# A four-part graph kernel on one core: pad rows only where they are read, block counts early in the table, gathers eight groups ahead, and edge rows inside the adding loop

## The reference, cut to what matters

```python
# relational layer, twice: one matrix of 20 per edge type, built from 8 bases
W   = jnp.einsum('rb,bio->rio', a, V)
seg = dst * R + etypes
agg = jax.ops.segment_sum(x[src], seg, num_segments=N * R).reshape(N, R, -1)
h   = jnp.einsum('nri,rio->no', agg, W) + x @ w_loop + bias
# plain sum
out = jax.ops.segment_sum(x[src], dst, num_segments=N)
# flow layer: a two-layer MLP per edge, forwards and backwards
fwd = mlp([x[future], x[past], edge_attr]);  fwd_agg = segment_sum(fwd, future)
bwd = mlp([x[past], x[future], edge_attr]);  bwd_agg = segment_sum(bwd, past)
out = mlp([fwd_agg, bwd_agg])
# attention over the edges of a node, 4 heads of 8
```

## Time and profile before

| what | us |
|---|---|
| runs | 3404.99, 3411.47, 3412.61 |
| median | 3411.47 |
| the profiled execution | 3402.48 |
| its span | 3400.5 |
| sort, to its last scatter | 843.2 |
| adding loop's stage | 851 to 986.5 |
| message table again, second relational layer | 986.5 to 1484 |
| sum layer | 1484 to 1889 |
| flow layer's pipeline | 1889 to about 2650 |
| attention | 2717 to 3400 |

### The profile page before, as it was taken

The page is one execution under the profiler, slowest core; times in us unless marked ns, Lnnn a source line. Parts: engine busy times, 40 slices in busy tenths (PEclk is TensorE's granted clock), DMA queues, the critical chain, the costliest instruction groups (busy, mean ns, idle before and its releaser), DMA issues. The chain is left out here.

```text
span 3400.5 us, 58425 instructions
## 1 busy us (share of the span) xinstructions
PE 2791.8 (82%) x19728; PEld 1844.5 (54%) x19838; DVE 2957.7 (87%) x8386; ACT 653.1 (19%) x1566; POOL 2125.8 (63%) x2076
## 2 busy tenths in 40 slices
PE   5788889885669999969998799999999767777752
PEld 3455555553446777746665466666666533333321
DVE  5999999996857999979999688888888479999987
ACT  2110101100310000001111222222222133333320
POOL 0377777776005777757775677777775277777740
PEclk6798988987556888869999799999999778888875
DMA  9111111110412111121111100000001011111120
GB/s 256 58 35 35 34 36 35 34 36 21 132 60 72 25 25 24 19 25 28 29 29 19 16 11 11 11 11 11 11 11 9 11 27 27 27 28 27 27 16 5
DMA packets 133363, 116.09 MB, mean 34 GB/s; under 512 B 58505, under 2 KB 116941, under 8 KB 132957
## 3 DMA queue, kind: packets, MB, share of 16 engines
q0 software_dynamic: 65152, 44.96, 8.4%
q1 hardware_dynamic: 64332, 59.23, 7.0%
q10 hardware_dynamic: 3600, 8.19, 0.7%
HBM read 70.58 MB, written 41.65 MB: 33 GB/s over the span
## 5 line engine op out<-in xcount | busy, mean ns | idle before, releaser
L1628 POOL DMA_INDIRECT flow_x<-node_table,src_indices x440 | 539.3, 1226 | 228.9 <-issue 104.5
L706 PE MATMUL p_in_picked<-block_table 128*96 128x512 bf16 x1725 | 446.1, 422 | 106.4 <-DVE block_table L594 106.4
L594 DVE TENSOR_SCALAR block_table<-in_sources,node_numbers 128x512 bf16<-128x512 f16 x1725 | 520.0, 371 | 0.8 <-PE p_in_picked L706 0.6
L1998 POOL DMA_INDIRECT att_kv_rows<-kv_table,att_index x440 | 425.1, 966 | 141.4 <-issue 132.2
L1086 POOL DMA_INDIRECT rel_rows<-message_table,message_indices x320 | 322.7, 1008 | 300.2 <-POOLq L1303 203.0
L1770 PE MATMUL flow_acc_bwd<-flow_onehot_j,flow_by_q 128*128 128x270 bf16 (+1 forms) x2530 | 493.7, 325 | 7.1 <-issue 0.2
L414 POOL DMA_INDIRECT sorted_edges<-block_table,sorted_row x416 | 406.3, 977 | 147.8 <-issue 147.8
L706 PEld LDWEIGHTS p_in_picked<-block_table 128*96 128x96 bf16 x1725 | 229.5, 136 | 297.2 <-DVE block_table L594 93.6
L1379 POOL DMA_INDIRECT sum_rows<-node_table,src_indices x280 | 270.4, 966 | 111.3 <-issue 85.0
L2034 DVE TENSOR_REDUCE att_tile_max<-p_att_scores 128x4 f32<-128x512 f32 x440 | 284.2, 684 | 28.4 <-PE p_att_scores L2148 24.9
L1414 DVE TENSOR_SCALAR sum_source_onehot<-sum_sources,node_numbers 128x512 bf16<-128x512 f16 x1000 | 300.6, 367 | 0.0
(11 more groups left out here) (344 smaller groups left out, 4997.7 us busy)
## 6 DMA issues: line engine op xcount, KB each, us to landing
sorted_edges<-pad_rows SPq DMA_DIRECT2D x1, 11440.0 KB, 54.7
rel_rows<-sorted_edges SPq DMA_DIRECT2D x20, 572.0 KB, 3.8
in_sources<-source_rows_in SPq DMA_DIRECT2D x69, 128.0 KB
message_table<-message_rows ACTq DMA_DIRECT2D x25, 320.0 KB, 2.2
message_table<-message_rows SPq DMA_DIRECT2D x25, 320.0 KB, 2.1
flow_x<-node_table,src_indices POOLq DMA_INDIRECT x440
att_kv_rows<-kv_table,att_index POOLq DMA_INDIRECT x440, 2.5
sorted_edges<-block_table,sorted_row POOLq DMA_INDIRECT x416, 2.2
```

Of the source, the lines that this page charges most:

```text
L594: last = dve.tensor_scalar(which[g % 2][:, c, :], srcs[b][:], s["node"][:, c:c + 1], None, ALU.is_equal)
L706: last = pe.matmul(pp[g % 2][0:3 * F, 0:CW], hs[:, c].rearrange("p k f -> p (k f)"), which[g % 2][:, c, :], start=(c == 0), stop=(c == NB ...
L1628: pool.indirect_dma_start(out=X[b][:, t, 0:F], out_offset=None, in_=d["nodes"], in_offset=bass.IndirectOffsetOnAxis(ap=s["idx_src"][:, g * ...
L1998: pool.indirect_dma_start(out=KV[b][:, t, :], out_offset=None, in_=d["kv"], in_offset=bass.IndirectOffsetOnAxis(ap=ibuf[b][:, t:t + 1], ax ...
```

## The change

Six edits, in program order:

1. Pad rows are written by SyncE only for the 24 tiles from EC on. Every tile below EC holds edges, so pad rows are read there only in the last tile of a block. Those 25 tiles GpSimd fills by 25 indirect scatters of 128 rows, once VectorE has their row numbers (`last_row`).
2. `BESIDE` goes from 11 to 7: TensorE meets the counts behind the 14th product, the turned limits behind the 16th (one block later instead of two), the tile map behind the 18th. Two subtractions of h move from behind the rank arithmetic to the counts, five operations on tile numbers move behind the second group's comparisons.
3. `AHEAD` goes from 4 to 8, `SLOTS` from 6 to 10. Group 0 is weighed one round earlier, with its basis products directly behind its pick.
4. `block_limits` runs ahead of the adding loop instead of behind it.
5. `edge_rows` runs inside the adding loop, in four chunks of 128 tiles. ScalarE copies source and type out of each load, TensorE turns the chunk, ScalarE copies it out, SyncE stores it. The destinations are now stored too (`dst_rows`).
6. The flow layer no longer turns one-hots. SyncE loads the destinations of a group as a broadcast to all partitions, and VectorE compares them with the lane number, which gives the turned one-hot at once.

```diff
-CG, CP, SLOTS, RINGS = 6, 4, 6, 4
-AHEAD, BESIDE = 4, 11
+CG, CP, SLOTS, RINGS = 6, 4, 10, 4
+AHEAD, BESIDE = 8, 7
...
-                sp.dma_start(d["sorted"][0:T * P, :].rearrange("(p g t) w -> p g (t w)", p=P, t=PADS),
+                sp.dma_start(d["sorted"][0:T * P, :].rearrange("(p t) w -> p t w", p=P)[:, EC:T, :]
+                             .rearrange("p (g t) w -> p g (t w)", t=PADS),
...
+                pool.wait_ge(recs, 2)
+                pool.wait_ge(pad_ready, 1)
+                pool.wait_ge(pads, 16)
+                for b in range(NB):
+                    pool.indirect_dma_start(
+                        out=d["sorted"], out_offset=bass.IndirectOffsetOnAxis(ap=last_row[:, b:b + 1], axis=0),
+                        in_=pad[:, 0, :], in_offset=None).then_inc(s["padded"], 16)
...
-                pool.wait_ge(pads, 16)
+                pool.wait_ge(s["padded"], 16 * NB)
...
                 dve.tensor_tensor(cnt[:], run[:, 1:NB + 1], run[:, 0:NB], ALU.subtract).then_inc(counts_ready, 1)
+                w = Steps(dve, steps)
+                dve.wait_ge(h_ready, 1)
+                w.done(dve.tensor_tensor(s["xc"][:], s["h"][:], top(s["h"][:]), ALU.subtract))
...
+                w.done(dve.tensor_scalar(cnt[:], upto[:], -1.0, 0.0, ALU.add, ALU.max))
+                dve.tensor_scalar(last_row[:], cnt[:], first_row[:, 0:1], None, ALU.add).then_inc(pad_ready, 1)
+                dve.tensor_tensor(s["sq"][:], s["xc"][:], top(s["xc"][:]), ALU.subtract).then_inc(steps, 1)
...
                 for g in range(CN):
                     sources(g)
-                    if g >= 2:
+                    if g >= 3:
                         weigh(g - 2)
                     types(g)
-                    if g >= 2:
+                    if g >= 3:
                         messages(g - 2)
+                    if g == 1:
+                        tile_numbers()
+                        weigh(0)
+                        messages(0)
...
                     if n == 2 * BESIDE:
                         counts()
+                    elif n == 2 * BESIDE + 2:
+                        limits_turned()
                     elif n == 2 * BESIDE + 4:
-                        limits_turned()
-                    elif n == 2 * BESIDE + 6:
                         tile_map()
...
+                        act.copy(edges["type"][:, mine], rows[b][:, :, TYPE])
+                        act.activation(edges["src"][:, mine], rows[b][:, :, SRC], ACT.Identity, bias=negmid[:, 0:1])
+                        act.copy(s["rec"][:, mine, :], rows[b][:, :, 0:REC]).then_inc(rec_taken, 1)
+                        if c - 1 in chunk_after:
+                            edges["act"](act, chunk_after[c - 1])
...
                     dve.memset(zeros[:], 0.0).then_inc(zero_ready, 1)
+                    dve.memset(negmid[:], float(-MIDDLE)).then_inc(zero_ready, 1)
+                    limits["dve"](dve).then_inc(limits_taken, 1)
...
+                    limits["pe"](pe)
                     pe.wait_ge(zero_ready, 1)
...
-                    edges["pe"](pe)
-                    limits["pe"](pe)
+                        if c + 1 in chunk_after:
+                            if chunk_after[c + 1] == 0:
+                                pe.wait_ge(limits_taken, 1)
+                            pe.wait_ge(rec_taken, c + 1)
+                            edges["pe"](pe, chunk_after[c + 1])
...
+                    def turned_onehots(i, g, b):
+                        dve.wait_ge(lanes_in[b], 16 * i + 16)
+                        if g >= 2:
+                            dve.wait_ge(q_done, g - 1)
+                        dve.tensor_scalar(OT[g % 2][:].rearrange("p t e -> p (t e)"), lanes[b][:], s["lane"][:, 0:1],
+                                          None, ALU.is_equal).then_inc(ot_ready, 1)
...
-                    def onehots(i, g, b):
-                        act.wait_ge(ot_done, g + 1)
-                        act.copy(OT[:].rearrange("p t e -> p (t e)"), pOT[:, 0:G * P]).then_inc(ot_copied, 1)
...
-                    def turn_onehots(i, g, b):
-                        pe.wait_ge(hot_ready, g + 1)
-                        for t in range(G):
-                            last = pe.transpose(pOT[:, t * P:(t + 1) * P], hot[b][:, t, :], s["identb"][:])
-                        last.then_inc(ot_done, 1)
...
-                        pe.wait_ge(ot_copied, g + 1)
+                        pe.wait_ge(ot_ready, g + 1)
```

165 lines of the change are left out of this document (95 added, 70 removed).

## The result

The changed kernel takes 3368.95 us (median of 4 runs, 3367.41 to 3384.12), the kernel before 3408.45 beside it (4 runs). The ratio is 0.989 (0.986 to 0.993): faster, by 36 us by the ratio (25 to 47 by its interval) and by 40 by the medians. I had forecast 3352 from a base of 3411.5, a gain of 59.5, with a range of 3331 to 3372. On that base the ratio gives 0.989 x 3411.5 = 3375, outside the range; the median 3369 stands just inside it only because the kernel before ran 3 us faster beside it. So the direction was right and the size wrong: the gain is some two thirds of the forecast one, and the missing 20 us are what the experiments are about.

A forecast was written before the change was run, and what follows sets the result against it. VectorE and GpSimd were taken to bound the sort, level with each other, and TensorE the flow layer; gains 43 (sort) + 4.5 (edge rows, limits) + 12 (flow) = 59.5, so 3411.5 - 59.5 = 3352, range 3331 to 3372.

The forecast's parts named there:

- Pads and counts: Sort's start: small pad write and earlier counts bring rank arithmetic to 46.5, first comparison to 80, table out at 86.
- 25 x 1.27 = 32 ... it costs nothing: GpSimd's 25 pad scatters from about 45 us take 32 us, ending at 77 to 82, before the table is out.
- the cover of 4 us: Margin between the latest forecast end of the pads (82) and the table being out (86); 0.2 us more a pad uses it up.
- rival (3): Sort: VectorE's rank arithmetic holds up all 25 pads, about 6.2 us each; slower than before, 3458; chance 0.03.
- milder form: Sort: pad scatters held to 2 to 4 us each, whole kernel 3360 to 3405; chance 0.04.
- the 0.99 us subtraction with two SBUF inputs: Sort: two such VectorE subtractions (at 110.94) cost 0.99, gathers beside them 1.30 or less; used as evidence against held pads.
- Eight groups ahead: Sort loop: eighteen gathers before the first scatter at 109; sort ends at 800, gain 43 (38 to 48), lead itself adding nothing.
- VectorE ... and eight DMAs behind them, 10: 800: Sort's end: VectorE's last messages at 790, then eight GpSimd DMAs taking 10 us, so last scatter at 800.
- Edge rows and limits: Adding loop: 12 us saved at its end, 5 lost at the front, 2.5 to nine transposes; gain 4.5 (0 to 7).
- Flow: Flow layer: without the transposes TensorE's period of 6.88 shrinks by 0.11 us a group (0.02 to 0.23); gain 12 (2 to 25).
- The weight load that now hides behind the transposes may show: Flow layer: with the transposes gone, TensorE's weight load before the product may be exposed; no separate size given.

The follow-up runs named there:

- the pauses: Changed kernel, each of VectorE's 25 rank operations waiting for its own end: 3367.08 us; with lead four, three additions and comparisons also broken into runs of 5: 3338.40.
- the late counts: Changed kernel with the counts' product back behind the table's 22nd product (BESIDE 11): 3377.21 us, ratio 0.990.

## Why the prediction was right or wrong

**Pads and counts: right on VectorE, wrong on GpSimd.** First comparison 79.7 (forecast 80), rank arithmetic 46.2 (46.5), the table out at 86 (its last store landed at 85.1, and the first gather came at 85.7 and 85.9 where the pads were in time; forecast 86). The step that failed is "25 x 1.27 = 32 ... it costs nothing". They took 58, and the cover of 4 us that I called thin was overrun by 18. The rival (3) had the right mechanism, at 3% and with a wrong size: it took all 25 pads to be held, where one hold lasts to the end of the chain, so that four were held and 25 pads lost 26 us and not 123. Its milder form, at 4% and with pads of 2 to 4 us and 3360 to 3405 in all, is what came: 58.1 / 25 = 2.3 us a pad. Two readings misled me. I took the 0.99 us subtraction with two SBUF inputs as evidence against a hold; but what is held is GpSimd, not VectorE, and one short operation holds for its own length only. And I looked at the mean step of DMAs in a loop in which GpSimd never rests, where nearly none is caught. A slip beside it: behind the first ten gathers 130 are left, not 132, so 546 DMAs and not 548; it moves no figure of the forecast.

The rule of the Trainium skill that I left at a small chance (SBUF — State Buffer, "SBUF: two separate sides") says that the shared port pair is an exclusive lock, also for VectorE operations with two SBUF inputs against a GpSimd operation that reads SBUF, and that the second to come blocks. The 14.13 us pad agrees, and goes beyond it: the page speaks of one instruction, the pad was held to the end of 25 of them, which followed each other every 0.57 us.

**Eight groups ahead: wrong in the end's size.** "VectorE ... and eight DMAs behind them, 10: 800" should have been 14 behind the last but one message. The earlier trace rows could have warned: 843.16 lay 19.5 us behind 823.64. So of the 16.5 us by which the sort missed 800, 7.8 were never to be had by this floor (VectorE's last messages at 792.57 instead of 790 included). The other 8.7 are what GpSimd's chain adds: 45.6 + 575 x 1.272 + 38.5 for five held DMAs = 815.5 for the start of its last DMA. Without the holds this chain would end ahead of VectorE's floor. But no run took the holds away without moving that floor, so the 8.7 are worked out and not measured; the pauses brought the last scatter forward by 1.3 us with the lead of eight, and by 6.6 with four. That the lead gives nothing by itself was right; that its slots cost 3.1 at the boundary I didn't see: I never asked what the 7.9 us of that boundary are made of (5.5 are GpSimd's DRAIN, which takes 8.7 with ten slots). What the lead can do (fill GpSimd's waits once the holds are gone) is then lost to VectorE's floor.

**Edge rows and limits: right in sum, by two errors that cancel.** The front cost 5.0 (forecast 5). The end gave 13.2 (12). The nine transposes inside the loop cost 0.5 over the loop (first to last load's products 103.6, then 104.2) and not 2.5: they lie in TensorE's idle 2.0 to 2.9 us a load, which is 2.1 to 2.2 instead of 2.7 to 2.9 at the three loads with a chunk. So the stage gave 7.6, and 2.4 of it were lost in the message table behind it (76.0 us in place of 73.5), where TensorE's clock was 0.52 in place of 0.55 on average. In one kernel with the same edit, that with the late counts, it was 0.55 and the table took 73.4, so the 2.4 don't come with the edit alone. 5.2 in all, against 4.5 (0 to 7).

**Flow: the mechanism right, the size half.** The product started 0.11 us sooner, as forecast from the copy's end. "The weight load that now hides behind the transposes may show" was named and not priced: the product's step to the next addition grew from 0.91 to 0.96 and took 0.05 of it back. (6.88 - 6.82) x 110 = 6.3 instead of 12, inside the bounds of 2 to 25. So the term that was mis-sized is the 0.11 us a group; it came to 0.06. VectorE's idle went to 1.01, not 0.7: its new comparison (0.26 a group in the timeline's steps) pushed the one-hots on, but these took 0.73 instead of 0.92.

**Sum.** From the profiled executions: 16.3 of the 24.6 us that were short of 59.5 come from the sort, 3.1 from the boundary, 5.6 from the flow layer, less 0.7 of the adding loop, and 0.2 from stages that the change doesn't touch. I had also let the median follow from a base of 3411.5; with a fourth run it is 3408.5.

## What to carry to other kernels

Work given to an engine that stands idle isn't free: look at what the other engines do in that very stretch, and at the longest chain without a pause that it can collide with, not at mean durations from elsewhere. Where two engines are level, find the floor that each sets at the end by counting what stands behind its last product; an earlier start is only worth the distance to the other's floor. And after removing work from the engine that sets the pace, look at what it waits for next, and move independent work into that gap: here that gave 23.3 us in the layer, where the removal itself gave 6.4.
